# Sorting an edge list in the setup stage: 23 columns scattered by GpSimd and 368 through the matmul loop, in place of 191 and 200

## The reference, cut to what matters

```
def _L0_gnn_ref(x, values, row, col):
    msgs = values[:, None] * x[col]
    return jax.ops.segment_sum(msgs, row, num_segments=3125)
x = x + _L0_gnn_ref(_layernorm(x, axis=-1), edge_weight, src, dst)
```

## Time and profile before

| | |
|---|---|
| median of three runs | 7212.45 us |
| runs | 7198.43 to 7218.48 us |
| span of the profiled execution | 7219.8 us |
| TensorE busy | 4789.4 us, 66% |
| GpSimd busy | 3558.3 us, 49% |
| VectorE busy | 3404.9 us, 47% |
| ScalarE busy | 2369.8 us, 33% |
| mean granted TensorE clock | 0.739 of full speed |

### The profile page before, as it was taken

One profiled execution on the slowest core, in us unless ns is written; L12 is line 12 of the kernel. 1 busy time (PEld: TensorE's weight loads), 2 busy tenths in 40 slices (PEclk: granted clock), 3 DMA queues, 4 the chain that ended last, 5 costly groups with the idle time before them and its releaser, 6 DMA issues. The chain is left out here.

```text
span 7219.8 us, 95026 instructions
## 1 busy us (share of the span) xinstructions
PE 4789.4 (66%) x20505; PEld 3662.0 (51%) x20506; DVE 3404.9 (47%) x12261; ACT 2369.8 (33%) x8104; POOL 3558.3 (49%) x3712
## 2 busy tenths in 40 slices
PE   3286767776777677766677757776785446555797
PEld 0033434654566456555444556666663334333686
DVE  3296667344444344463666733333444445445412
ACT  2153443225677567632444421111220001000222
POOL 4505663456554455535466436666336663665121
PEclk6597887886766777768888865555797777777799
DMA  3002332323232223223322210001223332332455
GB/s 67 3 0 70 83 85 67 100 82 86 79 81 70 77 79 80 78 71 96 94 82 82 59 24 7 7 7 7 63 95 90 87 89 73 87 88 76 140 193 199
DMA packets 296057, 542.34 MB, mean 75 GB/s; under 512 B 85799, under 2 KB 179537, under 8 KB 295452
## 3 DMA queue, kind: packets, MB, share of 16 engines
q0 software_dynamic: 162784, 380.56, 20.0%
q1 hardware_dynamic: 119942, 146.53, 6.4%
q10 hardware_dynamic: 13110, 13.08, 0.5%
HBM read 473.61 MB, written 66.30 MB: 75 GB/s over the span
## 5 line engine op out<-in xcount | busy, mean ns | idle before, releaser
L1606 PE MATMUL psM<-G,S 128*128 x3328 | 1200.2, 482 | 846.1 <-DVE XN L1671 437.6
L1570 POOL DMA_INDIRECT G<-table_ones,ids x1176 | 1126.1, 958 | 1043.2 <-ACT ids L1526 701.3
L1606 PEld LDWEIGHTS psM<-G,S 128*128 128x128 f32 x3328 | 708.3, 236 | 1176.4 <-issue 1086.1
L1671 DVE TENSOR_TENSOR XN<-XN,psM 128x257 f32 (+1 forms) x1680 | 703.4, 419 | 838.8 <-remote 274.0
L1328 POOL DMA_INDIRECT G<-table_gat,ids x832 | 804.5, 967 | 588.0 <-ACT ids L1282 320.1
L1380 PE MATMUL psM<-G,S 128*128 128x260 f32 (+1 forms) x2744 | 890.4, 477 | 303.5 <-ACT G L1293 111.0
L1380 PEld LDWEIGHTS psM<-G,S 128*128 128x128 f32 x2744 | 687.4, 298 | 455.8 <-issue 241.2
L1402 DVE TENSOR_TENSOR acc<-acc,psM 128x260 f32 (+1 forms) x1384 | 452.6, 327 | 834.1 <-PE psM L1380 276.4
L1293 ACT ACTIVATE G<-G 128x64 f32<-128x64 f32 x3328 | 818.1, 333 | 14.4 <-issue 7.6
L1355 PE MATMUL psE<-AD,St 128*128 x2792 | 529.3, 318 | 367.9 <-ACT St L1286 229.3
L1355 PEld LDWEIGHTS psE<-AD,St 128*128 128x128 f32 x2792 | 545.7, 282 | 417.8 <-issue 395.6
(11 more groups left out here) (505 smaller groups left out, 7326.8 us busy)
## 6 DMA issues: line engine op xcount, KB each, us to landing
w1s<-in_L_ffn_W SPq DMA_DIRECT2D x32, 1024.0 KB
w2s<-in_L_ffn_W SPq DMA_DIRECT2D x32, 1024.0 KB
land<-out_by_choice SPq DMA_DIRECT2D x75, 256.0 KB, 3.3
G<-table_ones,ids POOLq DMA_INDIRECT x1176
G<-table_gat,ids POOLq DMA_INDIRECT x832
rows_by_token<-XN SPq DMA_DIRECT2D x20, 640.0 KB, 3.3
G<-table_ffn_gat,ids POOLq DMA_INDIRECT x540
table_ones<-XN SPq DMA_DIRECT2D x10, 640.0 KB
```

The lines of the kernel that those rows point to most:

```text
L1570: pool.indirect_dma_start(G[:, k % RG * EG + j, :], None, table, bass.IndirectOffsetOnAxis(ids[:, k % GB, j:j + 1], 0)).then_inc(gathered[ ...
L1606: nc.tensor.matmul(psM[:, j, 0:W], S[:, g, j, :], G[:, bass.ds(at[g * EG + j], 1), :].rearrange("p a w -> p (a w)"), start=True, stop=True ...
L1671: nc.vector.tensor_tensor(ab, ab, psM[:, n0 % EG, 0:W], ALU.add).then_inc(added, 1)
```

## The change

One number changes: the third argument of the list by source, the number of columns that GpSimd scatters.

```
@@ -106,7 +106,7 @@
 def program(nc, a, out):
-    LA = Edges("by_src", 50000, 191, 2, False)
+    LA = Edges("by_src", 50000, 23, 2, False)
     LB = Edges("by_dst", 50000, 0, 0, False)
     LF = Edges("by_ffn_dst", 65536, 96, 1, True)
```

## The result

| | before | after |
|---|---|---|
| median | 7198.48 us (6 runs, 7191.61 to 7218.48) | 7170.69 us (6 runs, 7153.82 to 7176.31) |
| span of the profiled execution | 7219.8 us | 7163.7 us |
| first gather of the next stage | 573.92 us | 528.31 us |

The ratio of after to before is 0.9946, 95% interval 0.9925 to 0.9966: half a per cent faster, 39 us by the ratio and 28 by the medians. Forecast were 7171 us, in a range of 7150 to 7196. This is the result on the chip of the first measurement.

What follows compares the result with a forecast made beforehand. Setup was taken as bound by handshakes slowed by a long scatter train, then by VectorE in the loop. -133.4 - 54.0 + 144.5 + 1.5 = -41.4 us gave 7178.4 us for the profiled span, 7171 for the median, range 7150 to 7196.

Steps and rivals of the forecast that it cites:

- The crawl: Setup, 88 to 342 us: slow handshakes between engines, ranking steps each 5.60 us and not 0.89, put down to a long scatter train.
- Rival 1: Setup: the slow handshakes belong to the second ranking itself, not the scatters; +92 to +146 us, 7304 to 7358; chance 0.05.
- The list by destination, -133.4: Second ranking in setup: at full speed once the scatters stop, ending at 144.2 us where it ended at 277.6.
- The tail: After the last scatter in setup: handshakes stay slow a while longer; taken as 3 us, bounds 0 and 22.
- The row of 32 scatters: Later stage, 3131 to 3175.65 us: last late ScalarE copy starts 2.2 us after the last scatter's end; used to size the tail.
- The first half turns, -54.0: First four half turns of setup's column loop: 13.8 us without scatters beside them, where they took 67.8.
- 42 added, +144.5: Setup's column loop: 42 more half turns at a mean of 3.44 us each, 144.5 us added.
- +1.5 for the clock: Start of setup's loop: TensorE's matmuls take 5.07 us a half turn at low clock; 1.5 us added, bounds 0 and 7.
- Rival 2: Setup's loop: the clock falls and TensorE binds at 5.07 us or more a half turn; +34 to +109 us; chance 0.04.
- The sum, -41.4: All of setup: -133.4 - 54.0 + 144.5 + 1.5 us, the loop ending at 462 us and not 503.7.
- rival 4: Setup: slow handshakes clear at once and half turns take 3.39 us; -50 us, or -55, 7157; chance 0.12.
- What is said to cost nothing: Setup: shorter L697, L703, L705 (at most 0.6 us), SyncE's queue and read back, GpSimd's final wait; later stages only moved.

## Why the prediction was right, point by point

*The crawl is the scatters'.* Shown for setup on slow chips in four ways: fewer scatters shorten it (23, 71), a later train moves it, a broken train ends it, and other GpSimd work doesn't make it. What the prediction called "a long train" is to be read as "without a break": 191 scatters in fours do no harm. On fast chips the same train does hardly any either. Rival 1 has its arithmetic right there, +139 us at the first gather where it had +92 to +146, but not its cause: it put the crawl down to the ranking itself, and on these chips there is no crawl. The page SBUF — State Buffer of the Trainium skill ("Who interferes with whom": DMA never contends with a compute engine, GpSimd is what VectorE holds up) describes those chips. The trace agrees there: a scatter beside the full loop can take 1.27 us of busy time (78.74 us for 62) and not 0.96, and VectorE is busy for all of it:

```profile
200.00:300.00 100.00, 86.67 (x468) 43.30 (x466) 100.00 (x467) 71.16 (x234) 78.74 (x62) 1.00 0.02 1
```

So one remark of the prediction was read from too little: GpSimd doesn't keep its 1.29 us whatever VectorE does. Beside this full loop 62 scatters in 100 us are 1.61 us apart; in the trace before, no scatter lay beside a full loop.

The slow chips don't follow the page: steps of 5.60 us against 0.88. By which way the scatters slow the others there isn't shown. The trace of before held nothing of another kind of chip, and the forecast is right for the kind that had been profiled only.

*The list by destination, -133.4.* It ended at 142.2 and not at 144.2: -135.4. The tail was sized at 3 us and is not to be seen (the step from 116.17 is already 0.88 us long). L354 came 1 us later than said. A tail there is, only not after 23 scatters: 9 us after 71, 17 and 22 us after the two trains of 191. The row of 32 scatters was the right neighbour to go by, and the size still a guess.

*The first half turns, -54.0, and 42 added, +144.5, with +1.5 for the clock.* Together 318 us were said for 92 half turns; they took 314.2, 3.415 each. One wait of 2.57 us for TensorE stands at the cold clock (0.50 granted from 142 to 148 us, 0.57 to 152), and the rest run at 3.39. Rival 2 falls: 0.99 was granted over all 314 us.

*The sum, -41.4.* The loop's end (456.4 for 462, from 503.7) is -47.3. That is nearer to rival 4 (no tail, half turns of 3.39 us), which came to -50: with the wait of 2.57 us added it is rival 4 that happened, which had a chance of 0.12. The third list took 1.7 us longer than before, which leaves -45.6 at the first gather. The profiled span is shorter by 56.1; the other 10.5 lie in later stages that run the same instructions. No run looked for them, and runs of one kernel on one chip lie up to 59 us apart, so I don't read anything into it.

*The number, 7171.* That it meets the measured 7170.69 to within a microsecond is luck. It starts from 7212.45, the median of the first three runs; from the median of all six, 7198.48, the same sum gives 7157. The gain forecast was 41 us; by the medians 28 were measured, by the ratio 39 (24 to 54), and by the first gather of the profiles 46.

*What is said to cost nothing.* SyncE's read back starts at 133.95 (at 321.15 before), long before the loop's end. The early loss at L325 stayed, as said. That this loss, 9 us, could be cured too, only the broken train showed.

*What the prediction did not ask.* It took the train as given and moved the work off it. The train's cost was not in the number of scatters but in their having no breaks. By the ratios, each measured on a slow chip, the wait after every 8 with 183 columns is worth 168 us where the change is worth 39, and it uses a semaphore that is there anyway.

## What to carry to other kernels

Where engines wait for "remote" or "issue" beside a run of indirect DMAs, first break the run with a wait for what has been issued and see whether the waits go, before any work is moved; then balance the split against the other path. Compare on more than one chip before such a change is kept: here the same edit is 0.5% faster on one kind and 2.4% slower on another, while the wait after every 8 costs 0.35% on either fast chip (with 191 columns) and gains 2.3% (with 183) on a slow one. Read how an engine is slow, idle with "remote" or busy with longer instructions, since the two have different causes.

## What the runs showed of the hardware that was not expected

- **Two kinds of chip.** The kernel before takes some 7200 us on two of the four chips and in the first measurement, and some 5915 on the two others, 1300 us apart, and only about 200 of that is setup's. The rest lies in the later stages. There the row of the aggregation's VectorE add, for the kernel before, on the slow chip of the first measurement and then on a fast one, is (busy, mean ns | idle before it, and what ended it):

```profile
L1671 DVE TENSOR_TENSOR XN<-XN,psM 128x257 f32 (+1 forms) x1680 | 703.4, 419 | 838.8 <-remote 274.0 <-DMA G<-table_ffn_gat,ids 225.4 <-PE psM L1606 182.2
```

```profile
L1671 DVE TENSOR_TENSOR XN<-XN,psM 128x257 f32 (+1 forms) x1680 | 703.7, 419 | 542.5 <-PE psM L1606 527.7 <-issue 2.2 <-DVE XN L1671 2.1
```

  The work is as long (703 and 704 us), the waits aren't, and "remote" isn't among the causes named on the fast chip. These stages gather with GpSimd's indirect DMAs. The same crawl may be behind the waits; no run put breaks there, so this isn't shown. The mean granted clock is lower on the slow ones as well, 0.739 against 0.812; in the ranking it was 0.50 on both, so it doesn't make the crawl, and whether it plays a part in the later stages is open. What makes a chip slow or fast is open, and so is whether it is the chip or its condition at the time.
- **How slow a handshake can get.** On a slow chip a step of the ranking, one exchange between TensorE and VectorE, costs 5.6 us beside the train; a half turn of the loop with several costs up to 45.
- **Memsets of 128x700 on GpSimd** make a group of four 128x416 f16 operations on VectorE 3.05 us long and not 1.03. Scatters on the same chip leave the group at a mean of 1.06 (191 in fours).
- **A tail.** On slow chips the slow handshakes outlast the last scatter by 9 us (71 scatters) to 22 us (191).
- **Open:** whether it is the landing, the pause or the lower pace that ends the crawl; how long a train may be on a slow chip (4 is clean, 8 nearly, 16 wasn't run there); and whether the 32-scatter trains of the later stages are worth breaking.
